# A gated cross-attention layer with top-2 experts on one core: expert tiles of two independently routed 128-row parts (88 for 106), early weight copies moved from GpSimd to SyncE's DMAs

## The chip, the cores and the metric

One Trainium2 chip, and of it one core. The metric is the device time of one execution in microseconds (us), the median of several runs. Engines are named as in the profile: PE (TensorE matmuls; PEld is its weight loads), DVE (VectorE), ACT (ScalarE), POOL (GpSimd), SP (SyncE, which computes nothing here and issues DMAs).

## The reference

```python
# x, ctx: (128 batches, 64 rows, 128)
x = x + tanh(g_xattn) * attention(media=ctx, latents=layernorm(x))   # 8 heads, keys from ctx and latents
xn = layernorm(x)
probs = softmax(xn @ Wr + br)             # 8 experts
top_p, top_i = top_k(probs, 2)            # two experts of each row, weighed by their probability
h = relu(xn @ W1[e] + b1[e])              # 128 -> 256
y = h @ W2[e] + b2[e]                     # 256 -> 128
x = x + tanh(g_ffn) * (sum of the two chosen y, each times its probability)
```

All in float32. The reference computes every expert for every row; the kernel only the two chosen ones, by sorting rows to experts.

## The kernel before, in words

**Slots.** All five engines run the same loop over slots `n`, from `FIRST` = -15 to `LAST`, and each engine's program does its share of slot `n` in a fixed order. Slots 0 to 127 each take one batch of attention (scores, softmax over a three-slot pipeline, values, L1030, L1038, L1049 on PE; L903, L909 on DVE; L601, L609, L621 on ACT; L546 on POOL). Eight batches are a group (512 rows); the work that belongs to a group (projection L1080, queries L954 to L956, the transposes, layernorm, router, row placement) is spread over the eight slots `s = n % 8` of the next groups by the table `SHARED`. So slots are unequal: `s = 2` holds the projection and is the longest. There is no barrier between slots; only semaphores.

**Experts.** Groups are joined into six chunks of 2, 3, 3, 3, 3 and 2 groups (`CHUNKS`). When a chunk is routed, POOL has scattered its normalised rows, two copies each, into DRAM (`sorted_x`, L491), one region for each expert. DVE's `list_tiles` counts the filled tiles of each expert, and makes a table with a row offset (row 0) and an expert number (row 1) for each tile. A tile is 256 rows of one expert. The number of tiles run is fixed: the most that padding could ask for, `TILES` = 15, 19, 19, 19, 19, 15, together 106.

**Where a tile runs.** `tile_slots()` gives each tile a slot, one per slot, none in slots with `s = 2` while attention runs. Chunks 0 to 3 run beside attention: slots 35 to 51, 59 to 79, 83 to 103 and 107 to 127. These 72 are the early tiles (`LATE` = 72). Chunks 4 and 5 run at slots 131 to 164, after attention ("the tail" below). A tile `i` in slot `n` does this:

- SP, slot `n-4`: `load_tile` (L413) loads its 256 rows to `xt`, at a row offset read from the table into a register. The offsets of eight tiles are read at once (L409, `AT_ONCE` = 8).
- POOL, slot `n-1`, for early tiles, or ACT, slot `n-1`, for late ones: `fetch_weights` copies the expert's 642 floats per partition from `wall` (all experts, in SBUF) to one of three buffers `wt` (L525 on POOL, L652 on ACT); it waits until tile `i-3` is finished (`y_done`).
- PE, slot `n-1`: `turn_tile` transposes the rows (L999); ACT copies them out as `xtT` (L629).
- PE, slot `n`: `hidden_tile`, two matmuls of 256 columns (L1010); then DVE adds b1 and clips at zero, one instruction for each half of the hidden width (`hs`, L915).
- PE, slot `n+1`: `output_tile`, four matmuls of 128 columns (L1019); DVE adds b2 (`y_sb`, L943), which gives `y_done`.
- SP, slot `n+2`: `store_tile` (L421) stores it to `sorted_y`.

Every float32 matmul shows in the profile as two MATMUL instructions (transposes as one).

In a slot SP works in this order: `store_tile` (which waits for `y_done`), `load_tile`, then the loads of the next group's inputs (L434, L435, L440) and the store of a finished group (L445). PE's order in a slot is: scores, transposes of the probabilities, `hidden_tile`, first shared work, values, `turn_tile`, second shared work, `output_tile`, third shared work. In the tail `turn_tile` comes first.

**Back home.** POOL gathers the outputs of a group once its chunk's tiles are all stored (`gather_rows`, L504, eight indirect DMAs for a group); DVE's `combine` adds them to `x1` (L889, L894), and SP stores the group.

Of the kernel before, what the change touches and what calls it, by code (L numbers as in the profile page):

```python
# [32 lines left out]
TILE = 256  # L33
J = ROWS // TILE

TILES = tuple((2 * c * TOK + E * (TILE - 1)) // TILE for c in CHUNKS)
# [6 lines left out]
PACK = 2 * D + 2 * D + 2 + D  # L43
# [18 lines left out]
AT_ONCE = 8  # L62
# [68 lines left out]
def flamingo(nc, x, ctx_in, g_xattn, g_ffn, gamma_m, beta_m, gamma_l, beta_l, Wq, bq, Wkv, bkv, Wo, bo,  # L131
# [5 lines left out]
    with ctx:  # L137
# [100 lines left out]
        wt = sb("wt", [P, WB, PACK])  # L238
        hs = sb("hs", [P, 2, 2, TILE])
# [82 lines left out]
        wt_early = sem("wt_early")  # L322
# [34 lines left out]
        def wait_tiles_read(eng, k):  # L357

            for b in range(XB):
                wait(eng, got_x[b], 16 * len(range(b, FIRST_TILE[k + 1], XB)))  # L360
# [16 lines left out]
        def _(sp):  # L377
            def weights(n):
# [11 lines left out]
                if n == 0:  # L390
                    sp.dma_start(wall[:, :, 0:2 * D], W1.rearrange("e d n -> d e n")).then_inc(got_experts, 16)
                    for c in range(2):
                        sp.dma_start(wall[:, :, (2 + c) * D:(3 + c) * D], W2[:, c * D:(c + 1) * D, :].rearrange("e p n -> p e n")).then_inc(got_experts, 16)
                        sp.dma_start(wall[:, :, 4 * D + c], b1[:, c * D:(c + 1) * D].rearrange("e p -> p e"),  # L394
                                     allow_slow_non_contiguous=True).then_inc(got_experts, 16)
                    sp.dma_start(wall[:, :, 4 * D + 2:PACK], b2.partition_broadcast(P)).then_inc(got_experts, 16)
# [3 lines left out]
            def load_tile(i):  # L400
# [5 lines left out]
                if t % AT_ONCE == 0:  # L406
                    first_rows.clear()
                    m = min(AT_ONCE, TILES[k] - t)
                    _, got = nc.values_load_multi_w_load_instructions(table[0:1, k, t:t + m], engines=(mybir.EngineType.SP,),  # L409
                                                                      min_val=0, max_val=E * ROWS - TILE)  # L410
                    first_rows.update(zip(range(i, i + m), got))
                wait(sp, xt_ready, i - XB + 1)
                sp.dma_start(xt[:, i % XB, :, :], xs[k % SETS][bass.ds(first_rows[i], TILE), :].rearrange("(a p) d -> p a d", a=2)).then_inc(got_x[i % XB], 16)  # L413
# [37 lines left out]
        def _(pool):  # L451
# [21 lines left out]
            nc.gpsimd.iota(begins[:, 0, :, :], [[ROWS, E], [TILE, J]], base=0, channel_multiplier=0,  # L473
# [34 lines left out]
            experts = {}  # L508

            def fetch_weights(i):  # L510

                k = CHUNK_OF_TILE[i]
                t = i - FIRST_TILE[k]
                if i == 0:
                    pool.wait_ge(got_experts, 16 * 6)
                if t == 0:
                    wait_shared(pool, shared_out, "table", LAST_GROUP[k], 0)
                if t % AT_ONCE == 0:
                    experts.clear()
                    m = min(AT_ONCE, TILES[k] - t, LATE - i)  # L520
                    _, got = nc.values_load_multi_w_load_instructions(table[1:2, k, t:t + m], engines=(mybir.EngineType.Pool,),
                                                                      min_val=0, max_val=E - 1)
                    experts.update(zip(range(i, i + m), got))
                wait(pool, y_done, i - WB + 1)
                nc.gpsimd.tensor_copy(wt[:, i % WB, :], wall[:, bass.ds(experts[i], 1), :].rearrange("p e n -> p (e n)")).then_inc(wt_early, 1)  # L525

            for n in range(FIRST, LAST + 1):
# [20 lines left out]
                if TILE_AT.get(n + 1, N_TILES) < LATE:  # L548
                    fetch_weights(TILE_AT[n + 1])

        @block.scalar
        def _(act):
# [84 lines left out]
            def fetch_weights(i):  # L637
# [3 lines left out]
                if i == LATE:  # L641
                    act.wait_ge(got_experts, 16 * 6)
                if i == LATE or t == 0:
                    wait_shared(act, shared_out, "table", LAST_GROUP[k], 0)
                if i == LATE or t % AT_ONCE == 0:
                    experts.clear()
                    m = min(AT_ONCE - t % AT_ONCE, TILES[k] - t)
                    _, got = nc.values_load_multi_w_load_instructions(table[1:2, k, t:t + m], engines=(mybir.EngineType.Activation,),
                                                                      min_val=0, max_val=E - 1)
                    experts.update(zip(range(i, i + m), got))  # L650
# [30 lines left out]
        def _(dve):  # L681
            def weights(n):
# [9 lines left out]
                if n == FOLD_BIAS:  # L692
# [4 lines left out]
                    nc.vector.tensor_tensor(tg_bo[:, :], bo_sum[:, :], tg[:, 0:1], ALU.mult).then_inc(bias_ready, 1)  # L697

# [137 lines left out]
            def list_tiles(n, s):  # L836

                g = n // GB - 2
                if s == 1 and 0 <= g < G and g == LAST_GROUP[CHUNK_OF_GROUP[g]]:
# [23 lines left out]
                    nc.vector.tensor_scalar(gap[:, :], n_tiles[:, 0:E - 1], -float(TILE), float(ROWS), ALU.mult, ALU.add).then_inc(table_step, 1)  # L863
# [34 lines left out]
            def slot(n):  # L898
# [11 lines left out]
                if n in TILE_AT:  # L910
# [3 lines left out]
                    for c in range(2):  # L914
# [221 lines left out]
```

## Time and profile before

| | |
|---|---|
| median of 3 runs | 934.15 us (928.44 to 934.85) |
| the profiled execution | 935.25 us |
| its span, first to last instruction | 933.2 us |
| PE / DVE / ACT / POOL busy | 86% / 64% / 55% / 53% |
| mean granted PE clock | 0.964 |
| early tiles (72) | from 235 us to 797 us |
| tail (34 tiles) | hidden matmuls from 809 us to 899 us |

Busy is the time in which an engine executes something; matmuls are pipelined and their ends are modelled, so a busy PE is not PE at its peak. The chain of waits follows the work that ended last back to the start.

### The profile page before, as it was taken

How to read it: one execution, taken by the hardware profiler on the slowest of the kernel's cores; microseconds unless marked ns; L12 is line 12 of the kernel's file. 1: busy time of each engine (PE TensorE's matmuls, PEld its weight loads, DVE VectorE, ACT ScalarE, POOL GpSimd, SP SyncE). 2: the span in 40 equal slices, each digit the busy share in tenths (PEclk: the TensorE clock that was granted, in tenths of full speed). 3: DMA queues.
4: the chain of work that ended last, by engine and by line, in shares of the span. 5: the costliest groups of instructions: out<-in, count | busy, mean ns of one | idle time of the engine just before them, and what ended most of it. 6: DMA issues, size and time to landing. Idle time of an engine off the chain costs nothing.

```text
span 933.2 us, 15854 instructions
## 1 busy us (share of the span) xinstructions
PE 799.6 (86%) x4481; PEld 601.6 (64%) x4481; DVE 601.1 (64%) x1908; ACT 514.2 (55%) x1655; POOL 491.7 (53%) x510
## 2 busy tenths in 40 slices
PE   4757888788999898999899999989999989878750
PEld 4635556464778665777767686858587857568650
DVE  3515474846676947696958576868686758476661
ACT  3447566565757556666647575737575736334320
POOL 2103235253636347675344575747575756577555
PEclk9979999999999999999999999999999999989995
DMA  4963233102122112141212223322322222246552
GB/s 128 381 181 140 80 139 122 51 29 57 52 74 63 52 40 74 52 114 57 76 39 58 63 76 84 86 73 63 86 80 70 80 57 72 74 135 170 158 145 62
DMA packets 113976, 86.14 MB, mean 92 GB/s; under 512 B 11985, under 2 KB 104418, under 8 KB 113890
## 3 DMA queue, kind: packets, MB, share of 16 engines
q1 hardware_dynamic: 99618, 49.32, 19.1%
q0 software_dynamic: 8192, 16.79, 6.2%
q10 hardware_dynamic: 6080, 19.02, 5.1%
q8 instruction: 37, 0.61, 0.3%
q14 instruction: 49, 0.40, 0.1%
HBM read 39.74 MB, written 45.35 MB: 91 GB/s over the span
## 4 chain that ended last, share of the span: by engine, by line
PE 64%; DVE 10%; ACT 7%; issue 6%; POOL 5%; SPq 5%; DMA 3%; POOLq 0%; ACTq 0%; DVEq 0%
PE shared L1080 12%; PE batch L1049 11%; PE batch L1030 9%; PE hid_ps L1010 7%; PE y_ps L1019 6%; PE batch L1038 4%; ACT probs L601 3%; POOL yg L504 3%; PE shared L956 3%; PE shared L954 3%; PE shared L955 3%; ACT pT_sb L609 2%; DVE hs L915 2%; PE xt_ps L999 2%; SPq L394 1%
## 5 line engine op out<-in xcount | busy, mean ns | idle before, releaser
L546 POOL TENSOR_TENSOR probs<-probs,rsums 128x512 f32<-128x512 f32 x128 | 134.6, 1051 | 290.7 <-DVE rsums L909 289.4
L621 ACT ACTIVATE oT<-batch 128x512 f32<-128x512 f32 x128 | 76.6, 598 | 210.4 <-PE shared L1080 115.7
L601 ACT ACTIVATE probs<-batch,neg_max 128x128 f32<-128x128 f32 x512 | 180.9, 374 | 8.0 <-DVE neg_max L903 8.0
L903 DVE TENSOR_REDUCE neg_max<-batch 128x4 f32<-128x512 f32 x128 | 88.1, 688 | 120.1 <-PE batch L1030 118.9
L1049 PE MATMUL batch<-pT_sb,kvn 128*128 128x512 f32 x256 | 140.7, 631 | 24.4 <-ACT pT_sb L609 24.1
L1030 PE MATMUL batch<-kvT,qT 128*128 128x128 f32 x1024 | 142.9, 284 | 17.4 <-ACT oT L621 17.4
L1030 PEld LDWEIGHTS batch<-kvT,qT 128*128 128x128 f32 x1024 | 130.4, 195 | 42.0 <-ACT oT L621 28.7
L504 POOL DMA_INDIRECT yg<-sorted_y,home x128 | 126.5, 988 | 47.7 <-issue 31.9
L491 POOL DMA_INDIRECT sorted_x<-xn,row_of x128 | 130.9, 1023 | 32.3 <-issue 32.3
L1080 PE MATMUL shared<-oT,M 128*128 128x512 f32 x256 | 120.6, 615 | 0.8 <-ACT oT L621 0.8
L601 ACT ACTIVATION_READ_ACCUMULATOR probs<-batch,neg_max 128x1 f32 x512 | 110.1, 215 | 0.0
L664 ACT ACTIVATE qT<-shared,tb 128x512 f32<-128x512 f32 x128 | 87.8, 688 | 32.8 <-PE shared L956 26.2
L1019 PEld LDWEIGHTS y_ps<-wt,hs 128*128 128x128 f32 x712 | 92.4, 193 | 12.7 <-issue 9.1
L609 ACT ACTIVATE pT_sb<-batch 128x512 f32<-128x512 f32 x128 | 78.0, 609 | 37.8 <-PE batch L1038 36.4
L1010 PE MATMUL hid_ps<-xtT,wt 128*128 128x256 f32 x356 | 92.7, 383 | 6.3 <-ACT xtT L629 6.3
L1019 PE MATMUL y_ps<-wt,hs 128*128 128x128 f32 x712 | 95.8, 278 | 0.0
L915 DVE TENSOR_SCALAR hs<-hid_ps,wt 128x256 f32<-128x256 f32 x178 | 77.1, 475 | 26.6 <-PE hid_ps L1010 26.4
L1038 PE MATMUL batch<-ident,probs 128*128 128x128 f32 x512 | 79.8, 280 | 9.4 <-POOL probs L546 9.4
L943 DVE TENSOR_TENSOR y_sb<-y_ps,wt 128x256 f32<-128x256 f32 x89 | 37.2, 418 | 71.6 <-PE y_ps L1019 66.6
L1080 PEld LDWEIGHTS shared<-oT,M 128*128 128x128 f32 x256 | 48.9, 201 | 52.3 <-issue 52.3
L1049 PEld LDWEIGHTS batch<-pT_sb,kvn 128*128 128x128 f32 x256 | 40.0, 191 | 50.7 <-ACT pT_sb L609 43.3
L954 PE MATMUL shared<-latT_hi,A_hi 128*128 128x512 f32 x128 | 67.2, 525 | 3.4 <-ACT qT L664 2.4
(138 smaller groups left out, 1256.2 us busy)
## 6 DMA issues: line engine op xcount, KB each, us to landing
sorted_x<-yg ACTq DMA_DIRECT2D x36, 512.0 KB, 3.6
xt<-sorted_x SPq DMA_DIRECT2D x106, 128.0 KB
sorted_y<-y_sb SPq DMA_DIRECT2D x106, 128.0 KB
kv<-in_ctx_dram SPq DMA_DIRECT2D x16, 256.0 KB, 3.7
kv<-in_x_dram SPq DMA_DIRECT2D x16, 256.0 KB, 4.2
xres<-in_x_dram SPq DMA_DIRECT2D x16, 256.0 KB, 3.0
out_dram<-x SPq DMA_DIRECT2D x16, 256.0 KB
sorted_x<-xn,row_of POOLq DMA_INDIRECT x128, 2.4
```

Of the source, the lines that this page charges most:

```text
L491: nc.gpsimd.indirect_dma_start(xs[k % SETS][:, :], bass.IndirectOffsetOnAxis(ap=row_of[:, g, choice, c:c + 1], axis=0), xn[:, g % 2, c, :] ...
L504: nc.gpsimd.indirect_dma_start(yg[:, g % 2, c, choice, :], None, ys[k % SETS][0:TILES[k] * TILE, :], bass.IndirectOffsetOnAxis(ap=home[:, ...
L546: nc.gpsimd.tensor_tensor(pv, pv, rsums[:, m % 2, :].unsqueeze(2).broadcast_to([P, 4, P]), ALU.mult).then_inc(probs_ready, 1)
L601: last = nc.scalar.activation(probs[:, m % 2, c * P:(c + 1) * P], batch_ps[m % 3][:, c * P:(c + 1) * P], ACT.Exp, bias=neg_max[:, m % 2, c ...
L609: nc.scalar.activation(pT_sb[:, :], batch_ps[m % 3][:, :], ACT.Copy).then_inc(pT_done, 1)
L915: last = nc.vector.tensor_scalar(hs[:, i % 2, c, :], hid(i)[:, c * TILE:(c + 1) * TILE], wt[:, i % WB, 4 * D + c:4 * D + c + 1], 0.0, ALU. ...
L1010: last = nc.tensor.matmul(hid(i)[:, c * TILE:(c + 1) * TILE], wt[:, i % WB, c * D:(c + 1) * D], xtT[:, i % 2, :], start=True, stop=True)
L1019: last = nc.tensor.matmul(y_bank(i)[:, a * D:(a + 1) * D], hs[:, i % 2, c, a * P:(a + 1) * P], wt[:, i % WB, (2 + c) * D:(3 + c) * D], sta ...
L1030: last = nc.tensor.matmul(batch_ps[n % 3][:, c * P:(c + 1) * P], qT[:, g % 2, b, 2 * c:2 * c + 2, :].rearrange("p h i -> p (h i)"), kvT[:, ...
L1038: last = nc.tensor.transpose(batch_ps[m % 3][:, c * P:(c + 1) * P], probs[:, m % 2, c * P:(c + 1) * P], ident[:, :])
L1049: nc.tensor.matmul(batch_ps[m % 3][:, :], kvn[:, g % 3, b, :], pT_sb[:, :], start=True, stop=True).then_inc(o_ready, 1)
L1080: last = nc.tensor.matmul(sh[:, :], M[:, h, :], oT[:, h, :], start=(h == 0), stop=(h == H - 1))
```

## The change

- A tile is still 256 rows and one slot, but made of two parts of 128 rows (`HALF`). Each part has its own row offset and its own expert. The bound on tiles falls: `HALVES` = 23, 31, 31, 31, 31, 23 and `TILES` = 12, 16, 16, 16, 16, 12, together 88. The early ones are 60 (slots 35 to 47, 59 to 76, 83 to 100, 107 to 124), the late ones 28 (slots 131 to 158), and `LAST` falls from 179 to 173.
- The weights of a tile are now two packs, `wt[:, b, 2, PACK]`. For early tiles SP issues them as two SBUF to SBUF DMAs (128 partitions x 642 floats, 328,704 bytes each) in slot `n-1`, after `store_tile` and before `load_tile`. GpSimd's copies are gone. Late tiles have two ACT copies each in place of one.
- `load_tile` issues two DMAs of 128 rows. `AT_ONCE` is 4, so each table read still has eight values, but one is made every four tiles: for the rows by SP, for the experts by SP (early) or ACT (late).
- `hidden_tile` is four matmuls of 128 columns instead of two of 256. `hs` becomes one `max` of both parts with -b1 over 512 columns (DVE), and what this leaves out is put into b2: in slots 10 to 13 `fold_biases` adds W2 times b1 to b2 of all experts (16 matmuls of 128 columns on PE behind the work of slots 11 and 13; on DVE two copies of 1024 columns, two additions of 512, and a small negation).

```diff
-TILE = 256
-J = ROWS // TILE
-TILES = tuple((2 * c * TOK + E * (TILE - 1)) // TILE for c in CHUNKS)
+HALF = 128
+TILE = 2 * HALF
+J = ROWS // HALF
+HALVES = tuple((2 * c * TOK + E * (HALF - 1)) // HALF for c in CHUNKS)
+TILES = tuple((m + 1) // 2 for m in HALVES)
...
-AT_ONCE = 8
+AT_ONCE = 4
...
+        def read_table(engine, row, got, i, upto, biggest):
+            k = CHUNK_OF_TILE[i]
+            t = i - FIRST_TILE[k]
+            m = min(AT_ONCE - t % AT_ONCE, TILES[k] - t, upto - i)
+            _, values = nc.values_load_multi_w_load_instructions(table[row:row + 1, k, 2 * t:2 * (t + m)], engines=(engine,),
+                                                                 min_val=0, max_val=biggest)
+            got.clear()
+            got.update({(i + h // 2, h % 2): value for h, value in enumerate(values)})
...
                 if t % AT_ONCE == 0:
...
+                    read_table(mybir.EngineType.SP, 0, first_rows, i, N_TILES, E * ROWS - HALF)
                 wait(sp, xt_ready, i - XB + 1)
-                sp.dma_start(xt[:, i % XB, :, :], xs[k % SETS][bass.ds(first_rows[i], TILE), :].rearrange("(a p) d -> p a d", a=2)).then_inc(got_x[i % XB], 16)
+                for a in range(2):
+                    sp.dma_start(xt[:, i % XB, a, :], xs[k % SETS][bass.ds(first_rows[i, a], HALF), :]).then_inc(got_x[i % XB], 16)
+
+            def fetch_weights(i):
+                k = CHUNK_OF_TILE[i]
+                t = i - FIRST_TILE[k]
+                if i == 0:
+                    sp.wait_ge(experts_ready, 1)
+                if t % AT_ONCE == 0:
+                    read_table(mybir.EngineType.SP, 1, experts, i, LATE, E - 1)
+                wait(sp, y_done, i - WB + 1)
+                for a in range(2):
+                    sp.dma_start(wt[:, i % WB, a, :], wall[:, bass.ds(experts[i, a], 1), :].rearrange("p e n -> p (e n)")).then_inc(wt_early[i % WB], 16)
...
                 if n - 2 in TILE_AT:
                     store_tile(TILE_AT[n - 2])
+                if TILE_AT.get(n + 1, N_TILES) < LATE:
+                    fetch_weights(TILE_AT[n + 1])
                 if n + AHEAD in TILE_AT:
                     load_tile(TILE_AT[n + AHEAD])
...
-                nc.gpsimd.tensor_copy(wt[:, i % WB, :], wall[:, bass.ds(experts[i], 1), :].rearrange("p e n -> p (e n)")).then_inc(wt_early, 1)
...
-                nc.scalar.activation(wt[:, i % WB, :], wall[:, bass.ds(experts[i], 1), :].rearrange("p e n -> p (e n)"),
-                                     ACT.Copy).then_inc(wt_late, 1)
+                for a in range(2):
+                    last = nc.scalar.activation(wt[:, i % WB, a, :], wall[:, bass.ds(experts[i, a], 1), :].rearrange("p e n -> p (e n)"),
+                                                ACT.Copy)
+                last.then_inc(wt_late, 1)
...
-                    for c in range(2):
-                        last = nc.vector.tensor_scalar(hs[:, i % 2, c, :], hid(i)[:, c * TILE:(c + 1) * TILE],
-                                                       wt[:, i % WB, 4 * D + c:4 * D + c + 1], 0.0, ALU.add, ALU.max)
-                    last.then_inc(hs_done, 1)
+                    nc.vector.tensor_tensor(hs[:, i % 2, :, :, :], hid(i)[:, :].rearrange("p (a c j) -> p a c j", a=2, c=2),
+                                            wt[:, i % WB, :, 2 * D:2 * D + 2].unsqueeze(3).broadcast_to([P, 2, 2, HALF]),
+                                            ALU.max).then_inc(hs_done, 1)
...
-                for c in range(2):
-                    last = nc.tensor.matmul(hid(i)[:, c * TILE:(c + 1) * TILE], wt[:, i % WB, c * D:(c + 1) * D], xtT[:, i % 2, :],
-                                            start=True, stop=True)
+                for a in range(2):
+                    for c in range(2):
+                        last = nc.tensor.matmul(hid(i)[:, (2 * a + c) * HALF:(2 * a + c + 1) * HALF], wt[:, i % WB, a, c * D:(c + 1) * D],
+                                                xtT[:, i % 2, a * HALF:(a + 1) * HALF], start=True, stop=True)
...
+            def fold_biases(n):
+                for half in range(2):
+                    if n == BIASES + 2 * half + 1:
+                        pe.wait_ge(b1_wide, 2 * half + 1)
+                        for e in range(4):
+                            for c in range(2):
+                                last = nc.tensor.matmul(hid_ps[:, e * D:(e + 1) * D], hs[:, e // 2, e % 2, c, :],
+                                                        wall[:, 4 * half + e, USED + c * D:USED + (c + 1) * D],
+                                                        start=(c == 0), stop=(c == 1))
+                        last.then_inc(b2_folded, 1)
```

## Rows read from the trace of the kernel before

**Rows 1.** The page: PE in 40 slices, and the chain's shares by engine

```profile
PE   4757888788999898999899999989999989878750
...
PE 64%; DVE 10%; ACT 7%; issue 6%; POOL 5%; SPq 5%; DMA 3%; POOLq 0%; ACTq 0%; DVEq 0%
```

**Rows 2.** The chain of waits, 552 to 600 us: start, us, engine, line

```profile
554.14 0.86 PE hid_ps L1010 x4
...
558.95 0.87 PE hid_ps L1010 x4
...
579.19 0.86 PE hid_ps L1010 x4
...
581.65 0.22 PE xt_ps L999 x2
...
582.57 0.89 PE y_ps L1019 x8
...
585.49 0.86 PE hid_ps L1010 x4
...
597.53 0.88 PE hid_ps L1010 x4
```

**Rows 3.** Timeline of PE: slots without a tile, with one, and a chunk's end

```profile
168.88 1.13 PE L1030 MATMUL batch<-kvT,qT 128*128 128x128 f32 x8 [0.78 <-ACT oT L621]
...
196.07 1.05 PE L1030 MATMUL batch<-kvT,qT 128*128 128x128 f32 x8
201.24 1.05 PE L1030 MATMUL batch<-kvT,qT 128*128 128x128 f32 x8
...
215.62 1.13 PE L1030 MATMUL batch<-kvT,qT 128*128 128x128 f32 x8 [0.78 <-ACT oT L621]
...
309.58 1.06 PE L1030 MATMUL batch<-kvT,qT 128*128 128x128 f32 x8
...
339.17 1.05 PE L1030 MATMUL batch<-kvT,qT 128*128 128x128 f32 x8
...
601.62 1.03 PE L1010 MATMUL hid_ps<-xtT,wt 128*128 128x256 f32 x4
```

**Rows 4.** Timeline of SP's DMA issues, 549 to 591 us

```profile
549.86 0.37 SPq L421 DMA_DIRECT2D sorted_y<-y_sb  x1
...
555.08 0.36 SPq L421 DMA_DIRECT2D sorted_y<-y_sb  x1
558.24 0.39 SPq L413 DMA_DIRECT2D xt<-sorted_x  x1
...
572.92 0.36 SPq L421 DMA_DIRECT2D sorted_y<-y_sb  x1
...
590.88 0.37 SPq L421 DMA_DIRECT2D sorted_y<-y_sb  x1
```

**Rows 5.** DMA issues of the page: KB each, us from issue to landing

```profile
sorted_x<-yg ACTq DMA_DIRECT2D x36, 512.0 KB, 3.6
...
xres<-in_x_dram SPq DMA_DIRECT2D x16, 256.0 KB, 3.0
```

**Rows 6.** Groups of instructions by line: busy us, mean ns, idle before

```profile
L525 POOL COPY wt<-wall 128x642 f32 x72 | 56.2, 780 | 12.5 <-issue 12.5
...
L652 ACT ACTIVATE wt<-wall 128x642 f32 x34 | 25.1, 738 | 52.3 <-DVE y_sb L943 49.6 <-issue 2.2
```

**Rows 7.** The tail: PE's timeline (L1010 rows), and the chain of waits

```profile
837.51 1.59 PE L1010 MATMUL hid_ps<-xtT,wt 128*128 128x256 f32 x4
...
847.72 1.13 PE L1010 MATMUL hid_ps<-xtT,wt 128*128 128x256 f32 x4 [1.58 <-ACT xtT L629]
...
898.97 1.03 PE L1010 MATMUL batch<-xtT,wt 128*128 128x256 f32 x4
...
857.69 3.12 DMA xt<-sorted_x
...
906.76 0.95 POOL yg L504
```

More of the change, by code:

```diff
@@ L42 @@
 CHUNK_OF_TILE = tuple(k for k in range(NCH) for _ in range(TILES[k]))
-PACK = 2 * D + 2 * D + 2 + D
+USED = 2 * D + 2 + D
+PACK = USED + 2 * D
+BIASES = 10
 LOAD = -15
@@ L321, in flamingo @@
         got_x = [sem(f"got_x{b}") for b in range(XB)]
-        wt_early = sem("wt_early")
+        b1_wide = sem("b1_wide")
+        b2_folded = sem("b2_folded")
+        experts_ready = sem("experts_ready")
+        wt_early = [sem(f"wt_early{b}") for b in range(WB)]
         wt_late = sem("wt_late")
@@ L359, in wait_tiles_read @@
             for b in range(XB):
-                wait(eng, got_x[b], 16 * len(range(b, FIRST_TILE[k + 1], XB)))
+                wait(eng, got_x[b], 32 * len(range(b, FIRST_TILE[k + 1], XB)))
         def wait_rows_scattered(eng, k):
@@ L645, in fetch_weights @@
                 if i == LATE or t % AT_ONCE == 0:
[L646 to L650, printed above, removed]
+                    read_table(mybir.EngineType.Activation, 1, experts, i, N_TILES, E - 1)
                 wait(act, y_done, i - WB + 1)
-                nc.scalar.activation(wt[:, i % WB, :], wall[:, bass.ds(experts[i], 1), :].rearrange("p e n -> p (e n)"),
-                                     ACT.Copy).then_inc(wt_late, 1)
+                for a in range(2):
+                    last = nc.scalar.activation(wt[:, i % WB, a, :], wall[:, bass.ds(experts[i, a], 1), :].rearrange("p e n -> p (e n)"),
+                                                ACT.Copy)
+                last.then_inc(wt_late, 1)
             def read_out(what, g, number, bank):
@@ L697, in weights @@
                     nc.vector.tensor_tensor(tg_bo[:, :], bo_sum[:, :], tg[:, 0:1], ALU.mult).then_inc(bias_ready, 1)
+            def fold_biases(n):
+                for half in range(2):
+                    mine = slice(4 * half, 4 * half + 4)
+                    if n == BIASES + 2 * half:
+                        dve.wait_ge(got_experts, 16 * 6)
+                        nc.vector.tensor_copy(hs[:, :, :, :, :].rearrange("p t a c j -> p (t a) c j"),
+                                              wall[:, mine, 2 * D:2 * D + 2].unsqueeze(3).broadcast_to([P, 4, 2, HALF])).then_inc(b1_wide, 1)
+                    if n == BIASES + 2 * half + 1:
+                        dve.wait_ge(b2_folded, half + 1)
+                        bias = wall[:, mine, 2 * D + 2:USED]
+                        nc.vector.tensor_tensor(bias, hid_ps[:, :].rearrange("p (e n) -> p e n", e=4), bias,
+                                                ALU.add).then_inc(b1_wide, 1)
+                if n == BIASES + 3:
+                    dve.wait_ge(b1_wide, 4)
+                    nc.vector.tensor_scalar(wall[:, :, 2 * D:2 * D + 2], wall[:, :, 2 * D:2 * D + 2], -1.0, None, ALU.mult).then_inc(experts_ready, 1)
             def normalise_kv(n, k):
@@ L936, in slot @@
                 keep_table(n, s)
+                fold_biases(n)
                 if n in COMBINE_AT:
@@ L1000, in turn_tile, with fold_biases @@
                 last.then_inc(xt_ready, 1)
+            def fold_biases(n):
+                for half in range(2):
+                    if n == BIASES + 2 * half + 1:
+                        pe.wait_ge(b1_wide, 2 * half + 1)
[5 more added lines that the diff above has]
+                        last.then_inc(b2_folded, 1)
             def hidden_tile(i):
@@ L1018, in output_tile @@
                     for c in range(2):
-                        last = nc.tensor.matmul(y_bank(i)[:, a * D:(a + 1) * D], hs[:, i % 2, c, a * P:(a + 1) * P],
-                                                wt[:, i % WB, (2 + c) * D:(3 + c) * D], start=(c == 0), stop=(c == 1))
+                        last = nc.tensor.matmul(y_bank(i)[:, a * D:(a + 1) * D], hs[:, i % 2, a, c, :],
+                                                wt[:, i % WB, a, USED + c * D:USED + (c + 1) * D], start=(c == 0), stop=(c == 1))
                 last.then_inc(y_ready, 1)
@@ L1055, in slot @@
                 use_shared(n, "c")
+                fold_biases(n)
             def use_shared(n, place):
```

45 lines of the change are left out of this document (12 added, 33 removed).

## Prediction

> **What bounds the kernel now.** I read the page's slices and its chain first: PE is at 8 to 9 tenths from slice 12 on, and PE holds 64% of the chain [rows 1]. Then the chain of waits over eight slots in the middle: it is one unbroken row of PE work, the tile's own part among it (0.86 us of hidden matmuls, 0.89 us of output matmuls) [rows 2]. So in slots with a tile PE is full, and whatever keeps PE waiting there is paid in full. In slots without a tile PE is not full; their length comes from the softmax chain over the engines. So a removed tile gives back less than its PE work, and I take the gain from slot lengths, not from matmul times. Next SP's issues [rows 4], because the change puts the weights there; and last the tail, where tiles follow each other without attention [rows 7]. The profiled execution took 935.25 us, 1.1 above the median of 934.15. A measurement of this kernel can tell about 1% (9.3 us) from no change.
>
> **1. Twelve early tiles fewer.** Chunk 0 loses the tiles of slots 48, 49 and 51. Slots 48 to 51 take 29.6 us (309.58 to 339.17), and slots 24 to 27, the same places without tiles and with the same table work, 27.2 us (168.88 to 196.07) [rows 3]: 2.4 us, and some 0.9 for the output matmuls (0.89, rows 2) that the last tile leaves to slot 52. That is 3.3. Chunks 1 to 3 lose the slots with s = 5, 6, 7. Such slots with tiles take 16.1 us (585.49 of rows 2 to 601.62), without 14.4 us (201.24 to 215.62) [rows 2, 3]: 1.7 each for chunks 1 and 2. In chunk 3 no queries are left beside the tiles, so PE is less covered; I take 2.4 (between 1.7 and the 3 x 1.97 of PE work, nearer to the row). Sum 3.3 + 3.4 + 2.4 = **-9**, range -7 to -12.
>
> **2. Matmuls in halves.** 1024 columns in eight instructions take 0.89 us, in four 0.86 [rows 2]. 60 early tiles on a full PE x 0.03 = **+1.8**. DVE's `hs` goes from two instructions to one over as many columns. It is not on PE's unbroken chain: nothing there, +-1. Adding b2 and storing are as before.
>
> **3. Folding the biases.** 16 matmuls of 128 columns are 32 instructions; at 0.89 us for eight that is 3.6 us, placed behind slots 11 and 13, which have no tile. If their idle time covers them the cost is 0. But output matmuls that stand behind such a slot (slot 52 above) lengthened it by all of their time. I take **+3** (0 to 4). DVE's copies lie in slots where DVE waits.
>
> **4. POOL's copies go.** 72 x 0.78 = 56 us of POOL [rows 6]. POOL is on 5% of the chain [rows 1], none of it in the unbroken row [rows 2]: **0** (0 to -4, at the end of attention, where its normalising stands behind gathers).
>
> **5. The early weights on SP: do they arrive?** Fetching tile i stands in SP's order behind the store of a tile that was just finished, so it starts when that store is issued, and must land before PE's hidden matmuls. The time between the two now [rows 2, 4]:
>
> - s = 0: 549.86 to 554.14, 4.3 us
> - s = 1: 555.08 to 558.95, 3.9
> - s = 4: 572.92 to 579.19, 6.3
> - s = 7: 590.88 to 597.53, 6.7
> - s = 3, 5, 6: as long as s = 7 or longer, and no read there but a chunk's first, when SP has nothing to store
>
> What is needed: the store's issue 0.4, register work 0.15, then two DMAs of 329 KB. 256 KB take 3.0 us from issue to landing, 512 KB 3.6 [rows 5]; the pair is 657 KB in two issues, 0.5 us apart. The second alone would land at 0.5 + 3.0 = 3.5, a straight line through both rows gives 3.9 for 657 KB. I take 3.5 and need 4.05. That is 0.2 too late at s = 1 and in time at s = 0.
>
> Every fourth tile, eight registers are read from the table first. Between the store at 555.08 and the next issue at 558.24 lie 3.16 us; less the store's 0.4 that is 2.8 for one read [rows 4]. Then 6.85 is needed. The tiles with t % 4 = 0, a chunk's first aside, stand at slots 39, 44; 63, 68, 72; 87, 92, 96; 111, 116, 120: four at s = 7 (0.2 late), four at s = 4 (0.6 late), three at s = 0 (2.6 late). With the other s = 1 slots (0.2 x 4; after a late s = 0 there is room): 0.8 + 2.4 + 7.8 + 0.8 = **+12**. As PE is full there, all of it is paid. Bounds: with 3.0 for the pair it is 7; with 4.5 (the 3.9 and some 0.6 for the gathers that run in these slots) 0.8 x 4 at s = 0, 0.4 x 4 at s = 1, 1.6 x 4 at s = 4, 1.2 x 4 at s = 7 and 3.6 x 3 make 27. SP's own work in a slot is 0.4 + 1.0 + 1.0 for store and two pairs of DMAs, and 5.2 with a read: it fits in all but the shortest, where no fetch follows.
>
> The Trainium skill (DMA: Bandwidth & Descriptors, Anatomy of one DMA) gives for a DMA from GpSimd 2.0 us and the bytes at 436 GB/s; 657 KB would be 3.5 us, the value taken. The same page (Latency and other measured facts) puts most of the fixed time down to the write receipt of the target memory, HBM's being the slowest. That rule speaks for faster landings from SBUF to SBUF. No row before has such a transfer, and what it would do is the first rival.
>
> **6. The tail.** It keeps 28 tiles of 34. From slot 139 to slot 164 there are 25 steps in 61.5 us (837.51 to 898.97) [rows 7], 2.46 us each. Tiles that nothing disturbs take 1.97 (0.86 + 0.89 + 0.22 for the transposes [rows 2]). What changes:
>
> - ACT copies twice. A copy takes 0.74 [rows 6], and ACT waits for `y_sb` before it (49.6 us over the tail), so it has room, but the copy lies on a path: `y_sb` of tile i-2, copies for i+1, `xtT`, hidden matmuls of i+1, output matmuls, `y_sb` of i. Now PE, not that path, sets two undisturbed steps (3.94 us); I put its slack at half a microsecond, and with 0.74 more it is 4.2 us for two tiles: 2.1 each.
> - ACT reads its registers every four tiles (2.8 us, of which some 1.7 stick out behind the time it waits), and so does SP, which then is late with the next store and load; already now one read of SP makes PE wait for a load (3.12 us [rows 7]). SP's read sticks out by about 2.4, the second load included. The two stand in neighbouring slots, so one largely covers the other: 2.4 for four tiles.
> - Three combines fall between slots 139 and 158, at 1.6 each as now (the wait at 847.72 [rows 7]).
>
> Slots 139 to 158: 20 x 2.1 + 5 x 2.4 + 3 x 1.6 = 59 against 61.5. Slots 131 to 138, where routing on DVE dominates, get some +2. The last output then comes about as early as before, relative to the tail's start, and what follows it (16 gathers from 906.76, the last combine) is the same; one combine that stood before it falls behind it, -1.8. Sum **-2.3**, range -12 (if reads and copies hide, 6 tiles x 2.46 less what they add) to +6 (if ACT's and SP's reads add up).
>
> **Sum.** -9 + 1.8 + 3 + 0 + 12 - 2.3 = +5.5 on 935.25 is 940.8; less 1.1 for the median, **940 us**. What the fewer tiles give is eaten by PE waiting for weights.
>
> **Rivals.**
>
> - *The weights arrive in time.* If SBUF to SBUF lands in 2 us or so (this is where the page's receipt rule leads), and the read is short, term 5 is nearly 0: -9 + 1.8 + 3 - 2.3 = -6.5, so 928 us. With a better tail it reaches 918. For it: ranges of 4 to 7 us are of the size of the need. Against it: at s = 0 a read and even 1 us of landing make 0.55 + 2.8 + 1.5 = 4.9 us, over the 4.3 there.
> - *SP is the new bound, slower.* Landings at 4.5 us in bursts, and in the tail the reads of ACT and SP one after the other: slots 139 to 158 become 20 x 2.1 + 5 x 1.7 + 4 x 2.6 + 3 x 1.6 = 66, the tail +4.5 + 2; term 5 at 18. Then -9 + 1.8 + 3 + 18 + 6.5 = +20, 954 us. It decides as soon as the pair needs more than about 4 us to land. For it: SP's queue now has six DMAs a slot and two reads in four slots. Against it: DMA engines are idle most of the time.
> - *POOL's relief counts.* If normalised probabilities come earlier in slots without a tile, some 4 to 8 us more are gained than in the first rival: 921 us. Against it: term 4.
>
> **Chances.** Forecast (933 to 947) 0.45; weights in time 0.25; SP the bound 0.25; POOL's relief 0.05. Faster by over 1% (below 925): 0.45 of the first rival, the last, and a little of the forecast, 0.17. Slower by over 1% (above 943.5): most of the second rival and a third of the forecast, 0.37. Within 1%: 0.46. The range 924 to 958 leaves out the best of the first and the worst of the second rival. The likeliest one's own range is 933 to 947.
>
> **What would show it.** The hidden matmuls of slots 72, 96 and 120 should start some 2.6 us late, behind the landing of `wt<-wall`, and PE should wait there for that DMA, about 12 us in all; slots 5 to 7 of each group before a chunk's start should be 14.4 us long; slots 11 and 13 longer by 1 to 2 us; the tail from its first to its last hidden matmul about 89 us, as before, with ACT's and SP's reads in it. The forecast is wrong if PE's waits for `wt` sum to under 4 us or over 20, or if a tail tile takes 2.2 us or 3.5.

## The result, and the profile after

The changed kernel took **935.65 us** (median of 20 runs, 933.98 to 942.95), the kernel before 932.12 (20 runs beside them). The ratio is 1.0045, with an interval of 1.0027 to 1.0062: within the 1% that the prediction called no change, and in truth a little slower. The profiled execution took 935.37 us with a span of 933.6, where the profile of the kernel before has 933.2; so the two profiles differ by 0.4 us and the medians by 3.5. The prediction of 940 us stood 4 us too high.

The page of the changed kernel (the span, busy time by engine, PE in 40 slices, SP's DMA queue `q1` with packets, MB and share, then the chain's shares):

```profile
span 933.6 us, 16478 instructions
PE 774.2 (83%) x4613; PEld 587.8 (63%) x4613; DVE 558.0 (60%) x1771; ACT 520.6 (56%) x1659; POOL 440.9 (47%) x438
...
PE   4747988788999897999988999989899979778750
...
q1 hardware_dynamic: 108514, 84.06, 28.8%
...
PE 64%; ACT 9%; issue 7%; DVE 6%; POOL 5%; SPq 5%; DMA 3%; ACTq 0%; POOLq 0%; DVEq 0%
```

Against [rows 1] PE keeps its 64% of the chain. PE, DVE and POOL all have less to do (PE 799.6 us before, DVE 601.1, POOL 491.7), and the span is the same: what was removed was given back as waiting. Where, the waits of PE between 233 and 797 us tell (us in total, times, the longest):

```profile
PE shared L1142 <- DVE gap L891: 11.5, 4, 4.0
PE hid_ps L1050 <- issue: 11.4, 10, 2.4
PE batch L1089 <- ACT pT_sb L622: 10.6, 19, 1.1
PE batch L1070 <- ACT oT L634: 10.3, 15, 0.8
```

The second group did not exist before. `L1050` are the hidden matmuls, and what they wait for is a DMA landing, `wt<-wall`; the profile can name no engine for it, so it says "issue". The first group is older than the change and will matter below; in the kernel before it reads

```profile
PE shared L1101 <- DVE gap L863: 11.1, 4, 2.9
```

A late tile looks like this, first in SP's queue and then on PE (slot 96, s = 0, with a read of the experts' table, eight registers, ahead of its fetch):

```profile
603.24 0.38 SPq L453 DMA_DIRECT2D sorted_y<-y_sb  x1
606.34 1.15 SPq L445 DMA_DIRECT2D wt<-wall  x2
...
608.78 0.46 SPq L453 DMA_DIRECT2D sorted_y<-y_sb  x1
609.39 1.17 SPq L445 DMA_DIRECT2D wt<-wall  x2
```

```profile
606.46 1.06 PE L1070 MATMUL batch<-kvT,qT 128*128 128x128 f32 x8
607.35 0.60 PE L1078 MATMUL batch<-ident,probs 128*128 128x128 f32 x4
609.92 1.13 PE L1050 MATMUL hid_ps<-xtT,wt 128*128 128x128 f32 x8 [1.97 <-issue]
```

From the store's issue to the fetch's are 3.10 us with the read (603.24 to 606.34) and 0.61 without (608.78 to 609.39). From the first fetch's issue to the hidden matmuls are 3.58 us. These are the rows that answer to [rows 2, 4].

The fold of the biases lies where it was put (slot 11 here; slot 13 has the same two rows again):

```profile
106.92 1.95 PE L1036 MATMUL hid_ps<-wall,hs 128*128 128x128 f32 x16
108.70 1.06 PE L1070 MATMUL batch<-kvT,qT 128*128 128x128 f32 x8
```

The tail, answering to [rows 7]: first and last hidden matmul, and in the chain of waits what sets the end.

```profile
815.52 1.06 PE L1050 MATMUL hid_ps<-xtT,wt 128*128 128x128 f32 x8
...
898.72 1.16 PE L1050 MATMUL batch<-xtT,wt 128*128 128x128 f32 x8 [1.90 <-ACT xtT L642]
```

```profile
868.27 0.35 DVE y_sb L971
868.64 0.38 SPq L453
869.06 0.53 SPq L390
873.02 0.43 SPq L479
873.50 2.52 DMA sorted_y<-y_sb
876.04 0.70 issue
876.74 0.94 POOL yg L538
...
926.14 2.43 DMA yg<-sorted_y,home
```

The 27 steps take 83.2 us. The end hangs on something else: `y_sb` of slot 146 (the last tile of its chunk) starts at 868.27 and takes 0.35 us, but SP stores the tile before (868.64), reads eight registers (from 869.06, `L390`), loads a tile and stores a finished group (873.02, `L479`), and only at 873.50 comes its store. Behind it GpSimd runs the 40 gathers of the last five groups, 1.25 us apart, from 876.74 to 926.14.

### The profile page after: what moved, and what is told of

Read it like the earlier page. It is cut to its first block, busy times and chain, and to the rows that moved or that the text cites. A ratio compares the mean times of both kernels' runs of the same rounds, so it can differ in the third digit from the quotient of the medians.

```text
span 933.6 us, 16478 instructions
## 1 busy us (share of the span) xinstructions
PE 774.2 (83%) x4613; PEld 587.8 (63%) x4613; DVE 558.0 (60%) x1771; ACT 520.6 (56%) x1659; POOL 440.9 (47%) x438
## 4 chain that ended last, share of the span: by engine, by line
PE 64%; ACT 9%; issue 7%; DVE 6%; POOL 5%; SPq 5%; DMA 3%; ACTq 0%; POOLq 0%; DVEq 0%
PE batch L1089 12%; PE shared L1121 11%; PE batch L1070 10%; PE hid_ps L1050 6%; PE y_ps L1059 5%; PE batch L1078 4%; ACT probs L614 4%; POOL yg L538 4%; PE shared L984 3%; PE shared L982 3%; PE shared L983 3%; ACT pT_sb L622 2%; SPq L415 2%; ACT oT L634 2%; PE xt_ps L1027 1%
## 5 line engine op out<-in xcount | busy, mean ns | idle before, releaser
L614 ACT ACTIVATE probs<-batch,neg_max 128x128 f32<-128x128 f32 x512 | 180.4, 373 | 11.5 <-DVE neg_max L931 11.5
L525 POOL DMA_INDIRECT sorted_x<-xn,row_of x128 | 133.6, 1043 | 32.3 <-issue 31.6
L1121 PE MATMUL shared<-oT,M 128*128 128x512 f32 x256 | 119.2, 610 | 0.8 <-ACT oT L634 0.8
L1050 PE MATMUL hid_ps<-xtT,wt 128*128 128x128 f32 x592 | 81.1, 281 | 16.0 <-issue 11.4
L1050 PEld LDWEIGHTS hid_ps<-xtT,wt 128*128 128x128 f32 x592 | 73.2, 195 | 20.0 <-issue 13.5
L1059 PEld LDWEIGHTS y_ps<-wt,hs 128*128 128x128 f32 x592 | 76.6, 194 | 10.5 <-issue 8.1
L1121 PEld LDWEIGHTS shared<-oT,M 128*128 128x128 f32 x256 | 48.3, 198 | 51.8 <-issue 51.8
L1059 PE MATMUL y_ps<-wt,hs 128*128 128x128 f32 x592 | 80.2, 279 | 0.0
L942 DVE TENSOR_TENSOR hs<-hid_ps,wt 128x512 f32<-128x512 f32 x74 | 51.0, 690 | 37.0 <-PE hid_ps L1050 34.8
L1078 PEld LDWEIGHTS batch<-ident,probs 128*128 128x128 f32 x512 | 61.4, 144 | 14.3 <-POOL probs L561 14.3
```

The lines of the kernel that those rows point to most:

```text
L525: nc.gpsimd.indirect_dma_start(xs[k % SETS][:, :], bass.IndirectOffsetOnAxis(ap=row_of[:, g, choice, c:c + 1], axis=0), xn[:, g % 2, c, :] ...
L614: last = nc.scalar.activation(probs[:, m % 2, c * P:(c + 1) * P], batch_ps[m % 3][:, c * P:(c + 1) * P], ACT.Exp, bias=neg_max[:, m % 2, c ...
L1050: last = nc.tensor.matmul(hid(i)[:, (2 * a + c) * HALF:(2 * a + c + 1) * HALF], wt[:, i % WB, a, c * D:(c + 1) * D], xtT[:, i % 2, a * HAL ...
L1059: last = nc.tensor.matmul(y_bank(i)[:, a * D:(a + 1) * D], hs[:, i % 2, a, c, :], wt[:, i % WB, a, USED + c * D:USED + (c + 1) * D], start ...
L1078: last = nc.tensor.transpose(batch_ps[m % 3][:, c * P:(c + 1) * P], probs[:, m % 2, c * P:(c + 1) * P], ident[:, :])
L1121: last = nc.tensor.matmul(sh[:, :], M[:, h, :], oT[:, h, :], start=(h == 0), stop=(h == H - 1))
```

## The experiments

Each kernel is the changed one with the edit shown, unless it says otherwise, and each ran 4 to 10 times. "The table's matmul" is TensorE's transpose of the list of tiles, `("table", -2, 0, "c")` in `SHARED`. Ratios are to the kernel before. The first four ran on one chip and the next four on a second, each beside 19 runs of the kernel before at 932.3 and 932.1 us, so their times can be compared; the last four on a third chip, where the kernel before took 985.13 us, so of them only ratios compare.

**The experts' table is read a slot early.**

```
 def fetch_weights(i):
-    if t % AT_ONCE == 0:
+    if t == 0:
         read_table(mybir.EngineType.SP, 1, experts, i, LATE, E - 1)
 ...
     load_tile(TILE_AT[n + AHEAD])
+i = TILE_AT.get(n + 1, N_TILES) + 1
+if i < LATE and i not in FIRST_TILE and (i - FIRST_TILE[CHUNK_OF_TILE[i]]) % AT_ONCE == 0:
+    read_table(mybir.EngineType.SP, 1, experts, i, LATE, E - 1)
```

> The changed kernel, but SP reads the experts of the next four tiles one slot earlier, behind that slot's loads, instead of between the store and the weight DMAs (a chunk's first read stays). Theory 1 (PE is full in slots with a tile and waits for the weights because of the reads): in the changed kernel the waits for late weights sum to some 13 us, about 10.7 of them in tiles with a read; these go, and what is left is some 2.4 us in two tiles at s = 1. Time 7 to 11 us below the changed kernel (less if PE's clock dips return in slots 74 and 122, where they were absent), so 925 to 929 against 932 of the kernel before. Theory 2 (SP is too busy in any order): the read then delays the next store and fetch as much, the time stays within 3 us of the changed kernel's 936.

928.25 us, ratio 0.9942 (0.992 to 0.9963): 7.4 us under the changed kernel. Of PE's waits for weights

```profile
PE hid_ps L1053 <- issue: 4.0, 4, 1.4
```

is left. Slots 72, 96 and 120 fell from 7.0, 7.0 and 7.1 us to 4.8, 4.8 and 4.5; slots 44, 68 and 92 from 6.9 and slot 116 from 7.7, all to 6.3. What is left is elsewhere: slot 41 waits 1.4 us, slot 73 1.3 and slot 113 1.0. So the read ahead of the fetch is the greater part of the loss, and the time without it is what the rival "the weights arrive in time" gave (928).

**The early weights copied by GpSimd again**, two copies a tile, with its own read:

```
-sp.dma_start(wt[:, i % WB, a, :], wall[:, bass.ds(experts[i, a], 1), :]...)
+nc.gpsimd.tensor_copy(wt[:, i % WB, a, :], wall[:, bass.ds(experts[i, a], 1), :]...)
```

> The changed kernel, but the early weights come by two GpSimd copies per tile (as one before), not by SP's DMAs; the table is read by GpSimd every four tiles. Theory 1: no wait for weights' landing; SP is relieved; GpSimd has 2 x 0.78 us more per early tile (94 us in all) and a read of 2.8 us every fourth. If GpSimd has room, the time falls by the same 10 to 13 us, to 923 to 926. Theory 2 (GpSimd was near its limit in slots with scatters, 2.5 us of scatter, 1.05 of normalising, 1.0 of power, 1.6 of copies, of 6.3): its normalised probabilities come late and PE waits for them: 940 or more. I hold 2 for possible at s = 0, 1, 7, where two gathers (2.5), 1.05 and 1.6 are 5.2 us in slots of 4.3 to 4.8.

943.14 us, ratio 1.0115 (1.0082 to 1.0147), slower than with DMAs:

```profile
PE shared L1145 <- DVE gap L894: 14.0, 4, 4.0
...
PE hid_ps L1053 <- issue: 9.1, 11, 2.2
PE shared L1111 <- DVE kvn L742: 3.3, 5, 1.3
```

The waits for weights hardly fall (9.1 for 11.4 us), and two other groups grow: the list of tiles (14.0 for 11.5) and `kvn` (3.3 for 0.4). The time is that of the second theory, but its mechanism is not: in this stretch PE waits only 0.2 us for the normalised probabilities. Moving the weights to SP was worth 7.5 us against this version: the transfer costs, GpSimd would have cost more.

**As many tiles as before**, 106, the added ones empty:

```
-TILES = tuple((m + 1) // 2 for m in HALVES)
+TILES = tuple((2 * c * TOK + E * (TILE - 1)) // TILE for c in CHUNKS)
```

> The changed kernel with the tile counts of before (15, 19, 19, 19, 19, 15 instead of 12, 16, 16, 16, 16, 12), the extra ones empty. Output complete. It prices the removed tiles alone. Theory 1: 12 early tiles cost 9 us by the slots' lengths (range 7 to 12) and some more waits for weights (reads at slots 48 and 79, some 2 us); 6 tail tiles cost 6 x 2.1 to 2.8 = 13 to 17 us unless GpSimd's gathers hide them. Together 955 to 962. Rival (the end is set by GpSimd's chain of gathers, not by the tail's tiles): only the part of the tail before chunk 4's end counts, 3 tiles, and 948 to 952 result.

964.59 us, ratio 1.0318 (1.0272 to 1.0364): 29 us over the changed kernel, more than the 955 to 962 us expected. In the profiled execution, of 967.61 us, the loop is 21.7 us longer (the scores of slot 127 start at 819.5 for 797.8), of which 6.3 are more waiting for weights

```profile
PE hid_ps L1050 <- issue: 17.7, 13, 2.6
```

and what follows the loop 10.6 us. So 18 tiles are worth 29 us with the new way of fetching, 1.6 each: an early tile also carries a fetch that can be late. Read the other way, this kernel and the kernel before run the same 106 tiles, and the new form of a tile costs 32 us; leaving out 18 tiles pays back all but some 3 of them.

**Without the fold** (the output lacks W2 b1):

```
-bias = wall[:, mine, 2 * D + 2:USED]
-nc.vector.tensor_tensor(bias, hid_ps[...], bias, ALU.add)
 ...
-fold_biases(n)
```

> The changed kernel without folding b1 into b2: the 16 matmuls and the four DVE instructions of slots 10 to 13 are left out, so W2 times b1 is missing from the output. Theory 1: slots 11 and 13 fall from 6.7 and 6.9 us to 4.9 and 5.2, slots 12 and 14 rise from 4.5 and 4.0 to 5.2 and 4.6: 2.4 us less in all. Rival (the idle time of those slots covers it): under 1 us.

937.31 us, ratio 1.0051 (1.0018 to 1.0084). Slots 11 to 14 fell from 22.2 to 19.9 us, 2.3 us (the 2.4 expected is 2.2 by its own figures), but the time did not: other slots (41, 44, 65, 96, 120) and the start vary by as much from one execution to the next. The fold's cost in time stays open here.

One of these variations is worth a look. Slot 96 is the same code in both kernels, and PE waits there about as long for the weights (1.97 us above, 2.13 here). But it is 7.0 us long in the changed kernel's profile and 8.8 here (start:end of the slot, length, busy us of PE, PEld, DVE, ACT, POOL, granted clock, DMA share, GB/s; the changed kernel first):

```profile
606.46:613.50 7.04, 5.07 (x43) 4.32 (x42) 5.00 (x15) 3.66 (x15) 4.03 (x4) 1.00 0.82 263
```

```profile
608.62:617.46 8.84, 6.71 (x44) 5.30 (x43) 5.61 (x17) 4.40 (x19) 3.92 (x4) 0.81 0.70 224
```

Here the slot ran in part at the 1.2 GHz level (0.81 on average), and PE's work in it took 1.6 us longer. In the profiles of two later kernels that keep the read where it is, slot 96 is 8.8 us long too, with a wait of 2.0 and a clock of 0.80 and 0.81. So a late transfer sometimes has a second price, and the profile of the changed kernel happens to show none of it.

**SP's read of the first rows a slot early too**, on top of the first experiment (the same edit with `read_table(..., 0, first_rows, ...)` behind `load_tile`).

> The version with the experts read a slot early (928.25 us, span 925.5), and besides it SyncE's read of the tiles' first rows made a slot earlier too. Theory, that the end is set by when GpSimd can begin the 40 gathers behind the store of slot 146: a read of 2.8 us no longer stands between y of that slot and its store, so the store, the gathers and the end come up to 3 us earlier: 923 to 927 us. Rival, that GpSimd waits for the table's other users or for a combine anyway: 927 to 930 us, no difference from the read_early version.

927.5 us, ratio 0.9951 (0.9929 to 0.9972): no difference in time from 0.9942. In the profile the piece it was meant for did get shorter. From the tail's first hidden matmul to the end it took 115.5 us (812.3 to 927.8) for 119.7 (805.8 to 925.5); the loop before it happened to be 6.5 us longer in that execution.

**The table's matmul a slot later**, on top of the first experiment:

```
-    1: [("turn_kv", 1, 1, "a"), ("table", -2, 0, "c")],
-    2: [("project", -1, 0, "ab")],
+    1: [("turn_kv", 1, 1, "a")],
+    2: [("project", -1, 0, "ab"), ("table", -2, 0, "c")],
```

> The version with the experts read a slot early, and besides it TensorE's matmul for the tile table one slot later, behind the projection. Theory: in the changed kernel TensorE waits 11.5 us in 4 of them for VectorE's list of tiles, and the low granted clock behind such a wait costs another 1.7 us where a slot is 12.0 long in place of 10.3. Both go: 908 to 917 us, and the slots 50, 74, 98 and 122 are near 7 to 10 long. Rival, that VectorE's list delays the softmax of those slots and TensorE then waits for that: 923 to 929 us, the wait for VectorE only stands at another line.

907.33 us, ratio 0.9751 (0.971 to 0.9791), 21 us under the version without the edit. Between 233 and 797 us PE's waits no longer have the group:

```profile
PE batch L1092 <- ACT pT_sb L625: 14.1, 22, 2.0
PE batch L1073 <- ACT oT L637: 10.7, 16, 0.8
PE hid_ps L1053 <- issue: 5.1, 5, 1.6
...
PE shared L1124 <- ACT oT L637: 0.8, 1, 0.8
```

Slots 25, 49, 73, 97 and 121 fell by 3.0, 3.6, 2.5, 2.8 and 3.3 us, slots 26, 50, 74 and 122 behind them by 2.5, 1.7, 1.3 and 1.3.

**All three edits.**

> The experts and the first rows read a slot early, and the tile table's matmul one slot later. If the three costs add, it is the table_later version less up to 3 us: 905 to 916 us. If the end is bound by GpSimd's gathers alone, it equals the table_later version within 1 us.

905.0 us, ratio 0.9721 (0.9679 to 0.9764), the fastest with a complete output. The tail's first hidden matmul to the end is 112.3 us for 116.7 with the table's edit alone. The two times differ by 2.3 us, less than their intervals, but it is the second pair of profiles in which the first rows' edit took some 4 us from that piece.

**PE kept busy while it waits for the table.**

```
 elif what == "table":
+    for _ in range(22):
+        nc.tensor.transpose(sh[:, 0:P], ident[:, :], ident[:, :])
     pe.wait_ge(table_step, ...)
```

> The changed kernel with 22 transposes of the identity ahead of the tile table's matmul, so that TensorE is busy where it waited 2.4 to 4 us for VectorE. They are work without use. If the long slots 50 and 98 (12 us) are due to the clock that falls behind the idle time, they come down to about 10.3 as slots 74 and 122 are, and the granted clock behind the wait stays at 1.00: the time is 1 to 5 us under the changed kernel's 935.65. Rival, that the slots' length has another cause: the slots stay at 12 or grow by what the transposes outlast the wait, 935 to 940 us.

928.71 us, ratio 0.9961 (0.9932 to 0.9989), 6.9 us under the changed kernel, by adding work without use. Slots 26, 50 and 98 fell by 2.8, 2.4 and 1.7 us. The same stretch, first in the changed kernel and then in this one (start:end, length, busy us of PE, PEld, DVE, ACT, POOL, then the granted clock, DMA share, GB/s):

```profile
174.00:180.00 6.00, 4.07 (x25) 2.37 (x23) 5.65 (x19) 4.25 (x16) 1.64 (x2) 1.00 0.31 81
180.00:186.00 6.00, 3.94 (x15) 3.18 (x16) 3.99 (x15) 1.39 (x7) 0.46 (x1) 0.62 0.04 8
186.00:192.00 6.00, 6.00 (x13) 2.60 (x12) 2.18 (x6) 0.14 (x1) 2.90 (x3) 0.81 0.07 25
```

```profile
174.00:180.00 6.00, 5.54 (x40) 4.56 (x40) 5.54 (x22) 4.64 (x20) 1.04 (x1) 1.00 0.34 89
180.00:185.00 5.00, 4.33 (x21) 2.67 (x21) 4.35 (x13) 0.60 (x1) 1.79 (x2) 1.00 0.01 3
185.00:192.00 7.00, 6.25 (x21) 3.02 (x20) 0.70 (x4) 1.58 (x5) 1.57 (x2) 1.00 0.05 19
```

Behind the wait PE was granted 0.62 and 0.81 on average, that is the 1.2 GHz level for part of the stretch, and with the transposes 1.00. The dip is a cost of its own. That the three slots' sum is just the 6.9 us of the time is chance: in the same profile slots 72 and 96 grew by 4.4 and 1.7 us behind late weights, and slot 4 fell by 3.1.

**The kernel before with the table's matmul a slot later**, and nothing of the change.

> The kernel before, with TensorE's matmul for the tile table one slot later and nothing of the change. Theory, that this wait and the dip of the clock behind it are costs of both kernels, which the change neither brought nor took: the kernel before gains about what the changed one gained by the same edit (928.25 to 907.33 us), 908 to 916 us. Rival, that the new work (the early weights' reads on SyncE, the fold) made the wait: 925 to 933 us, no gain.

962.63 us, ratio 0.9777 (0.9741 to 0.9814): 22 us under the kernel before on this chip, as the changed kernel gained 21. So the wait is a cost of both kernels. And with it gone from both, the changed kernel with its three edits (956.22 us beside this one, ratio 0.9709) stands 0.7% below the kernel before with its one (962.63). No run of the one overlaps one of the other, but the difference is under the 1% that was called no change.

**Half of the last gathers** (the second expert's rows of groups 11 to 15 are not fetched):

```
-for choice in range(2):
+for choice in range(2 if g < 11 else 1):
```

> The changed kernel with one gather in place of two for each row of the last five groups, so 20 of the last 40 gathers are left out (and those rows' second expert is taken from what lies in the buffer). Theory, that GpSimd's gathers behind the store of slot 146 (40 of 1.25 us, back to back) set the end and not TensorE: the end is then set by the last y (901.9 us), its store, 8 gathers and the last combine, 920 to 925 us in the profile, 920 to 927 us in time. Rival, that the last y, its store and the output's transfers set the end: 932 to 936 us, no difference.

Ratio 0.9752 (0.971 to 0.9794), 957.96 us. It does not decide: the changed kernel itself did not run on this chip, and VectorE stood still several times in the tail there, so that slot 146 came later and GpSimd waited for it (at 904.76), and then for VectorE:

```profile
904.76 0.94 POOL L538 DMA_INDIRECT yg<-sorted_y,home  x1 [25.36 <-DMA sorted_y<-y_sb]
...
929.63 0.94 POOL L538 DMA_INDIRECT yg<-sorted_y,home  x1 [15.13 <-DVE x L922]
```

The last y and what follows it set the end there, not the queue of gathers. The price of a gather it does show: from the last y to the end are 20.3 us here (935.6 to 955.9) and 30.7 in the next kernel (923.3 to 954.0), 10.4 for eight gathers more, with the same 1.25 us between gathers as on the first chip.

**The three edits once more, and the same without the fold.**

> The version with the three edits (905.0 us, ratio 0.9721 to the kernel before) once more, beside the one without the fold on the same chip: 903 to 907 us.

> The same with no adding of W2 b1 to b2 (the biases of the hidden layer are left out of the output). If the fold costs what slots 11 to 14 show (2.4 us), 2 to 3 us under the other. If the first slots' waits vary by as much and absorb it: within 1 us of the other.

Ratios 0.9709 (0.9671 to 0.9747) and 0.9634 (0.9601 to 0.9667); 956.22 and 947.7 us. The times expected in microseconds were for the other chips. The loop was the same there (scores of slot 127 at 773.1 us, for 771.2), the tail some 50 us longer, with VectorE standing still. Its waits, in us, times and the longest, say "remote", and no row tells what that was:

```profile
DVE hs L948 <- remote: 30.4, 4, 13.0
...
DVE logit L810 <- remote: 9.2, 1, 9.2
...
DVE y_sb L977 <- remote: 7.8, 1, 7.8
```

Leaving the fold out gained 8.5 us there, more than the 2.3 of slots 11 to 14. Of the two profiles' 10.3 us, 5.1 are in the loop (2.3 in these slots, the rest spread over waits) and 5.2 in the tail, where VectorE's "remote" waits sum to 37.4 us and not 47.4. So both pairs of profiles show 2.3 us in the slots of the fold, while the times say 1.7 us more without it on the one chip and 8.5 less on the other; the surplus is not explained.

## Why the prediction was right

**1. Twelve early tiles fewer** (-9, range -7 to -12): measured **-6.5**, a smaller gain than the range allowed. Slots 76 to 80 and 100 to 104 fell by 1.4 and 1.3, for 1.7. Slots 5 to 7 of these groups are 15.3 us long, not the 14.4 named as a sign, since the last tile's output matmuls stand in slot 77 and 101. From slot 124 to the next projection (L1121, in slot 130) it is 2.9 less, for 2.4. The step that failed is chunk 0: slots 48 to 52 went from 35.7 to 34.8 us, 0.9 and not 3.3. Slots 48, 51 and 52 gave 1.7, but slots 49 and 50, which wait for the table and run at the low clock behind it, took 20.4 us for 19.6 before. I had taken slots 24 to 27 for the same place without tiles, and their length was itself a matter of such a wait: slots 25 and 26, without a tile in either kernel, took 18.2 us before and 19.9 after. Measured against 19.9, the 19.6 us of slots 49 and 50 with their tile show no cost of it at all.

**2. Halves** (+1.8): **0**. Slots 59 to 62, with tiles that no fetch delays, take 23.74 us in both kernels. That eight instructions are busy 0.03 us longer than four did not lengthen a slot.

**3. Fold** (+3): **+2.3**. Each half, eight matmuls in 16 instructions, takes 1.78 us (106.92 to 108.70), and slots 11 and 13 grow by that; but slots 12 and 14 behind them are 0.6 shorter each. So 2.3 of 3.6 us are paid, and the slots' own slack takes the rest.

**4. POOL's copies** (0): not seen as a gain. The version with GpSimd's copies shows the other side: two copies a tile cost 7.5 us more than the DMAs.

**5. Late weights** (+12): **+13.4** in the slots (2.2, 2.2 and 2.6 at s = 0; 0.7, 0.6, 0.7 and 1.4 at s = 4; 3.1 at slots 63, 89 and 113 together). The need was taken as 4.05 and 6.85 us, and is 0.61 + 3.58 = 4.2 without the read and 3.10 + 3.58 = 6.7 with it in the rows above. In the ten tiles where PE waited, the hidden matmuls start 3.55 to 3.58 us after the first fetch's issue in five (taken for the landing: 3.5), and 4.3 to 4.5 in the other five; the last are why slots 63, 89, 113 and 116 are later than forecast. An estimate by the formula in the Trainium skill (DMA: Bandwidth & Descriptors, Anatomy of one DMA), made there for one DMA from GpSimd, is also 3.5 us for 657 KB, and the five shorter ones agree. The faster landing in SBUF that I had drawn from what the Trainium skill says of write receipts (same page, Latency and other measured facts) did not show in these rows. The reads' part was shown by undoing it: 7.4 us of time. The 13.4 is of one execution; in others with the same reads, slots 72, 96 and 120 were another 1.6 to 1.8 us longer in six of nine cases, with the clock at about 0.8, and in one 4.4 longer.

**6. The tail** (-2.3, range -12 to +6): from its first hidden matmul to the end it went from 124.3 us to 118.1, **-6.2**. The first to the last hidden matmul takes 83.2 us, not the 89 that I named as a sign (90.1 before), and slots 139 to 158 take 52.5, not 59. From 139 to 158 there are 19 steps, and I had counted 20 (2.1 us). The 2.1 a tile held: ten of the steps take 2.10 to 2.24. The step that failed is the price of reads and combines, 5 x 2.4 + 3 x 1.6 = 16.8 us: the other nine steps are longer than these ten by 11.6 us in all. The end itself hangs on GpSimd's last 40 gathers in both kernels. They begin as long after the tail's first hidden matmul as before (61.2 us, before 61.3: 870.24 less 808.9), since SP's read stands ahead of slot 146's store. But they then run nearly without a pause (56.9 us from the first to the end of the span), where before they stood twice, for 2.3 and 4.5 us, ahead of a combine (63.0 us). In two pairs of profiles SP's read ahead of that store was worth about 4 us. In the five profiles of the changed kernel and its versions with early reads or a later table, the end comes 56.5 to 57.5 us after the first of the 40 gathers, while that first one comes anywhere from 55.4 to 62.2 us after the tail's start: so the end follows the gathers. No run without them shows it on these chips.

**Not in the sum.** Slots 74 and 122 took 10.3 us for 12.0, as no dip of the clock followed the wait before them (-3.4); slots 73, 97 and 121 took 1.0 less together, slots 25 and 26 1.7 more, slot 16 1.2 less, and the first eight slots ended 1.5 later. With these, the pieces give -6.5 + 2.3 + 13.4 - 3.4 - 1.0 + 1.7 - 1.2 + 1.5 = +6.8; the tail's first hidden matmul came 6.6 us later (808.9, now 815.5). The prediction had 7.8 for this piece.

So the mechanism was right, and part of the closeness is luck. The terms of the sum measured +3.0 for +5.5; POOL's apart they were off by 0.7 to 3.9 us, in both directions, and what was not in the sum took some 2.6 away again, which leaves the 0.4 us between the two profiles. The medians are 3.5 us apart.

The forecast's case held: 18 tiles fewer are paid for by weights that come late on a full PE. Of the rivals, "in time" gave the time that the kernel has with the read moved (928), and "SP is the new bound" was refuted by the tail, which got shorter, and its 18 us of late weights were 13.4. All of them missed the largest cost in sight, 11.5 us of PE's waits for VectorE's list with the dips behind them: it was in both kernels, so it moved no difference, but it is what stood in the way of a real gain.

## What to carry to other kernels

When work is taken from a full engine, look first at what its new supply has to come behind in an in-order queue: here a register read of 2.5 us in front of a 3.5-us transfer, moved one slot earlier, gave 0.8% of the time. Sort an engine's waits by sum before and after a change, those too that the change does not touch; moving one small matmul a slot later was worth 21 us, three times as much. And do not take a slot that is long by a wait as the measure of a place without work: slots 25 and 26 differed by 1.7 us between two kernels that do the same in them.

## What the runs showed of the hardware that I had not expected

A wait of PE for the table (2.4 to 4.1 us over all runs) can be followed by some microseconds at the 1.2 GHz level, and the slot behind it is then 11.6 to 13.1 us long in place of 10.1 to 10.3. It is not sure to: in one profile, that of the changed kernel, PE waited 2.37 us in slots 73 and 97 alike, and slot 74 then took 10.3 us and slot 98 12.0. The kernel before waited 2.69 us in slot 73, and the clock fell. These stretches, behind slot 73's wait, are the changed kernel and the kernel before, in the same columns as above:

```profile
473.00:477.00 4.00, 3.96 (x20) 2.57 (x21) 3.81 (x9) 0.60 (x1) 1.44 (x2) 1.00 0.22 73
```

```profile
465.70:470.00 4.30, 4.28 (x17) 3.04 (x18) 3.67 (x9) 0.60 (x1) 1.48 (x2) 0.60 0.59 152
```

The same happened behind waits for the weights of about 2 us: a granted clock of 0.81 over slot 96 in one execution, 1.00 in another. Useless transposes in the wait brought 6.9 us. And two chips ran the three edits' loop in the same time (773.1 and 771.2 us to slot 127's scores), and differed by 5.7% over the kernel (956.22 and 905.0 us); the 50 us lie in the tail, where VectorE stood still 47.4 us on the slower one. What held it is open.
